# Sharing the causal masks of an attention stage between VectorE and GpSimd

## The reference

```
x = x + global_latent_attn(rmsnorm(x, norm1_w), ...)
x = x + local_gqa_attn(rmsnorm(x, norm2_w), ...)
# global:
scores = einsum('bhqd,bhkd->bhqk', q, k) / sqrt(HD)
scores = where(i[:, None] >= i[None, :], scores, -1e30)
probs  = softmax(scores);  out = einsum('bhqk,bhkd->bhqd', probs, v)
```

## Time and profile before

| what | value |
|---|---|
| median of three executions | 1370.69 us |
| profiled execution | 1370.85 us |
| its span, first to last instruction | 1369.1 us |
| busy share of the span: PE, DVE, ACT, POOL | 86%, 72%, 60%, 32% |
| global stage, 76 to 430 us: PE, DVE, ACT, POOL busy | 302.5, 233.6, 298.0, 54.2 us of 354 |
| L905 in all | 80 instructions, 85.0 us |

### The profile page before, as it was taken

One profiled execution on the slowest core, in us unless ns is written; L12 is line 12 of the kernel. 1 busy time (PEld: TensorE's weight loads), 2 busy tenths in 40 slices (PEclk: granted clock), 3 DMA queues, 4 the chain that ended last, 5 costly groups with the idle time before them and its releaser, 6 DMA issues.

```text
span 1369.1 us, 36780 instructions
## 1 busy us (share of the span) xinstructions
PE 1176.2 (86%) x15602; PEld 698.9 (51%) x15602; DVE 987.5 (72%) x1573; ACT 821.8 (60%) x1218; POOL 437.6 (32%) x577
## 2 busy tenths in 40 slices
PE   3268888789888887867899999999999999999986
PEld 2123334344434554535566666666666666666653
DVE  4836765759575866869578777877778777877755
ACT  2179878788786664533555556455655566555641
POOL 1203030201013443665453333333433333333410
PEclk8579999999999998988899999999999999999997
DMA  3011302021021333110021011011110110111101
GB/s 97 5 38 44 124 29 85 18 92 32 17 94 32 125 109 109 48 45 18 17 76 26 21 26 26 21 25 26 29 26 22 25 26 22 27 24 26 29 6 62
DMA packets 37330, 59.79 MB, mean 44 GB/s; under 512 B 6416, under 2 KB 12464, under 8 KB 37168
## 3 DMA queue, kind: packets, MB, share of 16 engines
q1 hardware_dynamic: 37168, 57.44, 14.4%
HBM read 22.58 MB, written 16.78 MB: 29 GB/s over the span
## 4 chain that ended last, share of the span: by engine, by line
PE 46%; DVE 5%; issue 2%; ACT 1%; POOL 1%; DVEq 0%; POOLq 0%; ACTq 0%
PE psum L1229 8%; PE psum L1365 7%; PE psum L1318 5%; PE psum L1249 4%; PE psum L1340 4%; PE psum L1304 4%; PE psum L1239 4%; PE psum L1391 3%; DVE ffn_neg_max L1714 2%; PE psum L1289 1%; PE psum L1326 1%; PE psum L1295 1%; ACT ffn_hn L1570 1%; PE psum L1357 1%; PE psum L1261 1%
## 5 line engine op out<-in xcount | busy, mean ns | idle before, releaser
L742 ACT ACTIVATE att_probs<-psum 128x1024 f32<-128x1024 f32 (+2 forms) x384 | 355.8, 993 | 128.9 <-PE psum L586 127.3
L1661 POOL TENSOR_TENSOR ffn_rot<-ffn_rot,ffn_rot_sin 128x512 f32<-128x512 f32 x128 | 160.3, 1274 | 385.6 <-DVE ffn_rot L1692 385.6
L630 PE MATMUL psum<-att_probs,att_v 128*32 128x256 f32 (+3 forms) x3712 | 205.4, 349 | 2.2 <-DVE att_probs L905 1.3
L586 PE MATMUL psum<-att_q_stack,att_k_parts 64*128 64x512 bf16 (+4 forms) x1280 | 143.5, 299 | 43.6 <-ACT att_probs L742 28.6
L905 DVE TENSOR_TENSOR att_probs<-att_probs,att_causal_mask 128x1024 f32<-128x1024 f32 (+1 forms) x80 | 85.0, 1066 | 87.9 <-ACT att_probs L742 87.9
L630 PEld LDWEIGHTS psum<-att_probs,att_v 128*32 128x32 f32 x3712 | 97.0, 112 | 69.3 <-issue 40.5
L586 PEld LDWEIGHTS psum<-att_q_stack,att_k_parts 64*128 64x128 bf16 x1280 | 44.3, 95 | 146.4 <-ACT att_probs L742 88.6
L1543 ACT ACTIVATE ffn_max_t<-psum 68x128 bf16<-68x128 bf16 x64 | 17.4, 273 | 152.2 <-PE psum L1277 152.0
L1550 ACT ACTIVATE ffn_probs<-psum 128x1024 f32<-128x1024 f32 x64 | 65.6, 1025 | 59.2 <-PE psum L1304 59.2
L1512 ACT ACTIVATE ffn_sq<-psum 128x512 f32<-128x512 f32 x128 | 75.3, 594 | 27.9 <-PE psum L1229 27.7
L489 POOL TENSOR_TENSOR att_probs<-att_probs,att_local_mask 128x480 f32<-128x480 f32 (+1 forms) x48 | 61.9, 1295 | 79.9 <-ACT att_probs L742 79.8
(11 more groups left out here) (217 smaller groups left out, 2497.0 us busy)
## 6 DMA issues: line engine op xcount, KB each, us to landing
ffn_v_back<-ffn_v SPq DMA_DIRECT2D x120, 130.0 KB, 2.4
att_q_stack<-q_rows SPq DMA_DIRECT2D x28, 512.0 KB, 3.6
q_rows<-att_q_high SPq DMA_DIRECT2D x21, 256.0 KB, 4.5
q_rows<-att_q_mid SPq DMA_DIRECT2D x21, 256.0 KB, 4.2
q_rows<-att_q_low SPq DMA_DIRECT2D x14, 256.0 KB, 4.2
xres<-in_hidden SPq DMA_DIRECT2D x4, 512.0 KB, 4.3
out<-ffn_qk_t SPq DMA_DIRECT2D x3, 512.0 KB, 3.2
att_q_stack<-att_q_high SPq DMA_DIRECT2D x24, 32.0 KB, 2.0
```

The source lines that it names most:

```text
L586: ins = T.matmul(psum[:, banks[i] + at:banks[i] + at + width], k_parts[rows, p % 3, j, kt * P:(kt + 1) * P], q_stack[rows, turn % 2, j, q0 ...
L630: ins = T.matmul(psum[32 * g:32 * g + V_PAD, (4 + cc) * BANK + lo - cc * BANK: (4 + cc) * BANK + hi - cc * BANK], v[:, p % 4, kt, g, shift ...
L742: act.activation(probs[:, n % E_BUFS, 2 * j:2 * j + 2, 0:width], ps2((step % 2) * 2).rearrange("p (h c) -> p h c", h=2)[:, :, 0:width], AC ...
L1661: steps.did(pool.tensor_tensor(out, out, halves(k.rot_sin[:, n % 2, :])[:, :, 1 - half, :], ALU.add), g["added"] if half else None)
```

## The change

In the global stage GpSimd now masks heads 2 and 3 of each masked unit, and VectorE heads 0 and 1, each with the multiply of before on half of the heads: 128x256 for one block, 128x512 for two. The multiply has become a function that both engines call. GpSimd's multiply stands first in its tick, as the local one does, and waits for both exponentials of the unit. `values` waits for `masked` and for `masked_rest` in every masked unit, local or global. The local stage is computed as before.

```diff
-    def causal_blocks(n):
-        buf, blocks = probs[:, n % E_BUFS, :, :], diagonals(n)
+    def causal_blocks(n, h0):
+        buf, blocks = probs[:, n % E_BUFS, h0:h0 + 2, :], diagonals(n)
...
+    def hide_future(engine, n, h0):
+        blocks = causal_blocks(n, h0)
+        seen = keep.causal_mask[:] if len(blocks.shape) == 3 else keep.causal_mask[:].rearrange("p (o b) q -> p o b q", o=1)
+        return engine.tensor_tensor(blocks, blocks, widen(seen, list(blocks.shape)), ALU.mult)
...
             for n in range(FIRST_TICK, LAST_TICK):
-                if 0 <= n < n_units and phase_of(n) == 1:
+                if 0 <= n < n_units and is_masked(n):
                     pool.wait_ge(exp_done, STEPS * (n + 1))
...
+                    else:
+                        hide_future(pool, n, 2).then_inc(masked_rest, 1)
...
                     if is_masked(n):
                         pe.wait_ge(masked, masked_upto[n])
-                    if a == 1:
-                        pe.wait_ge(masked_rest, local_upto[n])
+                        pe.wait_ge(masked_rest, masked_upto[n])
...
-                        c.did(V.tensor_tensor(blocks, blocks, widen(seen, list(blocks.shape)), ALU.mult), masked)
+                        c.did(hide_future(V, n, 0), masked)
```

More of the change, by code:

```diff
@@ L417, in attention_stream @@
     masked_upto = [sum(is_masked(i) for i in range(n + 1)) for n in range(n_units)]
-    local_upto = [sum(phase_of(i) == 1 for i in range(n + 1)) for n in range(n_units)]
-    def causal_blocks(n):
-        buf, blocks = probs[:, n % E_BUFS, :, :], diagonals(n)
+    def causal_blocks(n, h0):
+        buf, blocks = probs[:, n % E_BUFS, h0:h0 + 2, :], diagonals(n)
         if len(blocks) == 1:
@@ L485, in _ @@
             for n in range(FIRST_TICK, LAST_TICK):
-                if 0 <= n < n_units and phase_of(n) == 1:
+                if 0 <= n < n_units and is_masked(n):
                     pool.wait_ge(exp_done, STEPS * (n + 1))
-                    rows = local_row(n, POOL_HEAD)
-                    pool.tensor_tensor(rows, rows, keep.local_mask[:, 0:width_of(UNITS[n][2])],
-                                       ALU.mult).then_inc(masked_rest, 1)
+                    if phase_of(n) == 1:
+                        rows = local_row(n, POOL_HEAD)
+                        pool.tensor_tensor(rows, rows, keep.local_mask[:, 0:width_of(UNITS[n][2])],
+                                           ALU.mult).then_inc(masked_rest, 1)
+                    else:
+                        hide_future(pool, n, 2).then_inc(masked_rest, 1)
                 for b in ln_due("shift", n):
@@ L901, in _ @@
                     else:
-                        blocks = causal_blocks(n)
-                        seen = keep.causal_mask[:] if len(blocks.shape) == 3 else keep.causal_mask[:].rearrange(
-                            "p (o b) q -> p o b q", o=1)
-                        c.did(V.tensor_tensor(blocks, blocks, widen(seen, list(blocks.shape)), ALU.mult), masked)
+                        c.did(hide_future(V, n, 0), masked)
                 for b in ln_due("stats", n):
```

## The result

The changed kernel took 1379.21 us (median of 5 runs, 1376.54 to 1383.27) against 1370.69 (5 runs beside it, 1365.3 to 1372.75): a ratio of 1.0068 [1.0049, 1.0087]. Forecast were 1378.5 and "slower". Its profiled execution took 1376.54 us, the fastest of the five, so the profile shows 5.7 of the 8.5 us; a second trace of the same kernel (`e1_again`) was taken in an execution of 1385.82 us.

What follows compares the result with a forecast made beforehand. PE and ACT were taken to bound the stage by turns, with DVE mattering only where someone waits for its last piece. Seven replays summed to 7.6 us over the profiled 1370.85, giving 1378.5 us; range 1367 to 1388 us.

Steps and rivals of the forecast that it cites:

- Step 1: Ticks 17 to 19: DVE and POOL masks alternate, L950 ends late and ACT's root near 124 us starts 1.3 us later.
- Step 2: Ticks 25 to 30: masks and the moved row square delay L868, so PE's transpose near 146 us comes 2.4 us later.
- Step 3: Before the PE stall at 192 us: four POOL masks and Newton among DVE work make L887 end 0.7 us later.
- Step 4: Before the PE stall at 259 us: masks 71 to 73 cost about 0.9, the square's leaving saves 1.9, net -1.0 us.
- Step 5: Before the PE stall at 370 us (L1066): mask 118 and POOL's later L509 push L943, +0.65 us.
- Step 6: Key copies L877 before 284 and 343 us: DVE late beyond its room, +0.45 and +1.3 us.
- Step 7: Before ACT's wait at 398 us: L504 and POOL masks 126 to 128 enter, L933 comes 1.8 us later.
- The clock rival: PE's clock falls behind a new stall near 146 us, +2 to 4 us once or twice: 1384 us, chance 0.17.
- The slack rival: Delays vanish in DVE's idle time and PE-bound gaps; replays 1, 2, 6, 7 give a fourth: 1373 us, chance 0.20.
- The relief wins: POOL yields the port, DVE keeps its savings, stalls at 192 and 259 us shrink: 1362 us, chance 0.09.
- replay 6: The same as Step 6: key copies before 284 and 343 us, +0.45 and +1.3 us.
- My 9.8 us by that rule: Sum if fast cast L870 also stands behind POOL masks, up to 1.1 us more at each key copy, instead of 7.6.

Runs made afterwards that it cites:

- e3: The changed kernel without POOL's multiplies and PE's wait for them, heads 2 and 3 unmasked in the global stage: 1358.86 us, 0.9913 of the kernel before.
- e9: e3 plus POOL multiplies of resident rows of x by the mask into a scratch tile nobody reads: 1382.28 us against 1371.37 for the kernel before.
- e10: The changed kernel with masks shared only in 22 units at ticks 10 to 16 of a phase: 1371.25 us against 1371.37 for the kernel before.
- e2: The kernel before, with POOL waiting for each masked unit's exponentials as in the change but masking nothing: 1372.37 us, 1.0019 of the kernel before.
- e4: The changed kernel with POOL's row square put back right behind Newton for phases 2 to 6: 1373.66 us, 1.0031 of the kernel before.
- e8: The kernel before, one row square held until DVE masked unit 73, POOL alone masking all heads of units 45, 46, 71: 1363.73 us, 0.9957.

## Why the prediction was right, and where its steps were off

The mechanism was right, and e3, e9 and e10 show it: where DVE's work is dense, POOL's multiplies make DVE stand for longer than the shorter masks save. The relief alone would gain 11.5 us, POOL's multiplies cost 20 to 25, and nothing where DVE has idle time. The number was right partly by offset, of the steps and of the clock. The lags between the places give each step; the first number is the first trace's, the second `e1_again`'s.

- **Step 1, ticks 17 to 19:** 1.3 forecast, 1.3 and 1.3 measured.
- **Step 2, ticks 25 to 30:** 2.4 forecast, 3.8 and 3.6. I had let both casts pass unheld, and L981 and L985 stood 0.4 and 0.95 us here. I also named the wrong first victim: PE waited for a mask of DVE, before the transpose, and behind that new stall the clock fell in both traces, so that 16 value matmuls took 1.63 and 1.93 us instead of 1.07. Of the step, the square's move is worth 1.4 us by itself (e2) but only some 0.5 when it is put back (e4), for then POOL's masks fill the same place.
- **Between steps 2 and 3** the lag fell by 0.7 and 0.4 us: at 157 PE had waited 1.26 us for a DMA of the queries, and coming later it waits 0.54 and 0.85. No step had this.
- **Step 3, before 192:** +0.7 forecast, -2.8 and -1.3. This is the step that failed in sign. The 0.7 us of DVE's lateness isn't there: from the mask that opens the stretch to the end of the copies, DVE needs 15.5 us in both kernels (rows below), as what L946, a mask and L953 stand is saved by other masks and by L959 (now L962). PE reaches the stall 5.8 us late and leaves it 4.6 us late, as late as it was at 184, because its scores had waited for exponentials on the way. So the stall of 3.05 us is 1.79 long and nothing has been won by its end. What is won comes behind it, by the clock: 1.00 and 0.88 over 190 to 200 us, where it had been 0.66.
- **Step 4, before 259:** -1.0 forecast, -4.4 and -2.0. The stall fell by 2.7 us rather than 1.0. In the first trace the clock also stayed up, in the second it fell.
- **Step 5, before 370:** 0.65 forecast, 1.9 and 3.1; the stall went from 1.99 to 2.81 us, 0.8 of the step, and half clock followed, which it hadn't before, for 3.4 us in the first trace and 6.8 in the second.
- **Step 6, key copies:** 0.45 forecast at 284, 2.1 and 2.3 measured. The wait grew by 0.85 us, behind two Newton steps that each stood 1.1 us, which no row of my replay had; the rest is half clock behind it. At 343 it was 1.0 and 1.0 of 1.3 forecast, but by a wait of 1.01 us for L973 at 329, not by the copy.
- **Step 7, before 398:** 1.8 forecast, 2.4 and 4.9. ACT waits 1.36 us for L936 instead of 0.18, as said, and beside it PE waits 2.40 us for a mask instead of 1.26; but another 1.1 us had arisen before, where PE waits for L973 at 394. In the second trace the clock fell again.

DVE before the stall of step 3, in the kernel before and then in the changed one:

```profile
176.42 0.91 DVE L905 TENSOR_TENSOR att_probs<-att_probs,att_causal_mask 128x512 f32<-128x512 f32 x1 [8.29 <-ACT att_probs L742]
190.70 1.27 DVE L887 COPY tail_space<-psum 128x512 f32<-128x512 f32 x2
...
181.05 0.64 DVE L428 TENSOR_TENSOR att_probs<-att_probs,att_causal_mask 128x256 f32<-128x256 f32 x1 [8.41 <-ACT att_probs L748]
195.26 1.28 DVE L893 COPY tail_space<-psum 128x512 f32<-128x512 f32 x2
```

The first trace ends the global stage 4.8 us late, the second 12.6; the forecast was 7.6. Undersized delays (steps 2, 5, 6, 7) and missed reliefs (3, 4) cancel. By the sums of 5 x (1 - clock), the clock gave the first trace 3.2 us against before and took 5.0 from the second (estimates); the sum of the forecast had neither, and that 1378.5 fell so close to the median is in part luck. The steps left out the clock as a term: each stall that grew or shrank also moved the speed of the matmuls behind it.

Signs announced and seen: roots near 124 and 402 waiting over 1 us, the shorter stall at 259. The wait for L868 near 146 wasn't seen, since the mask came first. The neighbours of the masks were to be longer by 20 to 40 us in total; L943, L970, L972, L980, L984 and L955 together gained 7.5 us, and DVE's own masks stood some 13 us. So DVE's busy time fell 13 us where I wrote "hardly". POOL's was 163 us in the stage (76 to 435), not 134: its masks alone would take 84 us, close to my 80, but a standing POOL instruction counts as busy, and the masks show 110. I had left that standing out.

The clock rival (0.17) wasn't a case beside the forecast but its spread: behind the new stall at 146 and the longer ones at 284 and 370 the clock fell in both traces, behind the shorter ones at 192 and 259 in the second alone. The slack rival is out by e3 and e9: DVE's time was worth 11.5 us one way and 20 or more the other. "The relief wins" failed as its condition said, since a POOL multiply once started makes DVE stand; its 2.2 us of excess at 259 stand in no row, have 1.7 (2.91 less 1.22).

The Trainium skill, "GPSIMD Engine Reference", section "Key points", lets DVE instructions in a two-port mode contend with GpSimd, beside those with two SBUF inputs. The rows agree for the cast L876 (L870 before): 0.69 us, and once 1.17, at 214. At the two key copies of replay 6, where I had weighed it, it gave nothing: L876 took 0.69 us at 274 and at 336. The casts L981 and L985 were held as well, but at 0.75 us for 768 columns against 0.69 for 1024 they aren't at the same pace, and no run here tells which mode they ran in. My 9.8 us by that rule were right in naming an undersized term, but put it at the wrong instructions.

## What to carry to other kernels

Moving an elementwise multiply from VectorE to GpSimd trades its duration against the holds between the two: whatever two-input instruction, cast or small tensor-scalar meets it may stand until it is through, and a short instruction can pay as much as a long one. Look at what runs beside it, piece by piece: here the move was free and worthless where DVE has idle time (e10), lost in dense stretches, and paid just ahead of points where somebody waits, beside reduces or PSUM reads (e8). Before spreading work, find the two or three stalls and shift those pieces alone (e8), and when summing later steps, start them from the delayed engines, not from the old times, and give each stall a range for the clock behind it.

## What the runs showed of the hardware

- **A hold doesn't get shorter with the instruction that it stops.** DVE's 128x8 multiplies went from 0.17 to 1.25 and 1.28 us, a 128x160 tensor-scalar from 0.24 to 1.31 (e8), beside POOL masks of 1.27 and 2.39 us. Reduces of 1280 columns kept 2.35 us, and copies from PSUM 0.68 us.
- **Both engines stand.** Where two masks were released together, DVE's often kept its 0.69 us and POOL's took 1.78 instead of 1.27 (at 271.6, for one). Over the stage POOL's masks took 110 us for 84 us of work and DVE's 60 for 47.
- **Casts stand too.** The 128x768 casts from SBUF to SBUF, of 0.75 us alone, reached 1.70 us (L985 at 143.56), and a 128x1024 one of 0.69 us took 1.17 (L876 at 214.43).
- **The same stall does or doesn't lower the clock.** PE's transposes behind stalls of 2.50 and 2.52 us ran at half and at full clock in two executions of one program. In e2 the matmuls behind 3.05 us took 1.13 us, where before they took 2.05 after the same 3.05. Here that makes up to 9 us between runs, and what sets it stays open.
- **POOL's multiply depends on its inputs.** Mask by mask, both inputs broadcast, took 0.61 and 1.04 us where real rows by the mask took 0.73 and 1.28.
